# Two-layer adaLN transformer and mixer on one core: the mixer's step size by one Softplus on ScalarE

## The chip, the cores and the metric

The kernel runs on one core of a Trainium2 chip, in one launch. The metric is device microseconds of that core, the median of several runs. The engines are named TensorE (PE), VectorE (DVE), ScalarE (ACT), GpSimd (POOL) and SyncE (SP).

## The reference, cut to what matters

There are 8 sequences ("batches") of 512 tokens of width 128. Layer 0 is attention and a mixture of experts; layer 1 is a mixer (a selective scan) and a second mixture of 8 experts. The mixer, for each batch, with 256 channels and 16 states:

```python
xc = silu(conv(x_in))                                   # (512, 256)
proj = xc @ x_proj_w + x_proj_b                         # (512, 48)
d_raw, Bm, Cm = split(proj, 3)                          # 16 each
delta = softplus(d_raw @ dt_proj_w + dt_proj_b)         # (512, 256)
dA = exp(delta[..., None] * A)
dBx = (delta * xc)[..., None] * Bm[:, :, None, :]
h = dA_t * h + dBx_t                                    # along the tokens
y = sum over n of h[n] * C[n]
```

## The kernel before

Each engine runs one program written out by hand, and the engines wait for each other on counting semaphores. Everything of a batch has its 128 features or channels on the partitions and its 512 tokens along the free axis; the 256 mixer channels are two halves c = 0 and 1. The loop runs over the batches b. In one pass the engines do the attention of batch b, its first experts, its mixer up to the end of the scan, and in the gaps of all this the second layer's experts of batch b - 1 ("behind": batch 0 has none to fill its gaps, and the last batch's come alone, after the loop, as the tail). `early(e)` stands for such pieces outside the scan; in the scan `SCAN_HIDDEN`, `SCAN_OUTPUT` (TensorE), `SCAN_GELU` (ScalarE) and `SCAN_ADD` (VectorE) fix after which step which piece comes. An expert's hidden chunk is one product on TensorE (`hid1`, L602) and one Gelu on ScalarE (`gelu1`, L933). `hid1(n)` waits for the Gelu of chunk n - 2, as two banks take turns.

The mixer's middle part, in which the change lies, goes like this. TensorE makes `proj`, which ScalarE copies out with its bias (L1063). From it start three things. SyncE stores 16 rows of B to DRAM (L398) and loads them back spread over all partitions, two rows (512 KB) in each of 8 DMAs p (L407), into the three slots of `b_wide`; p = 0 goes out at once, p = 1 waits for `dt_l`, because slots 0 and 1 lie in the space of `dt_exp` and `dt_abs`, and p = 2 stands behind it in SyncE's program. VectorE splits B and C into three bfloat16 parts (L1456 to L1458, L1462, L1463: `split_ok`). TensorE makes the input of the softplus for both halves (`dt_mm`, L849).

The softplus is max(z, 0) + ln(1 + exp(-|z|)): ScalarE does Abs (L1066), Exp (L1069) and Ln (L1072) for each half, and VectorE z itself (L1461) and max and sum (L1467). VectorE then has u = delta * xc (L1471).

The scan has 16 steps n of two halves. ScalarE makes the decay factors exp(delta * A) into PSUM (`decays`, L1078; three banks take turns, so decay k waits for scan k - 3). GpSimd makes the injections u * B (L445 for n = 0, L447 after that). VectorE runs the recurrence (L1482, "scan (n, c)") and the product with C (`read_product`, L1162), for which TensorE spreads row n of C (L872, queued behind the scan's wait for `split_ok`). GpSimd (L466) and TensorE (L663) add up the products. After decays 2, 7, 11, 15, 19, 23 and 27 ScalarE loads the Gelu table (L1084), does three Gelus (four after decay 2: chunks 12 to 15) and loads the Exp table again (L1087).

Of the kernel before, what the change touches and what calls it, by code (L numbers as in the profile page):

```python
# [23 lines left out]
ALU = mybir.AluOpType  # L24
# [17 lines left out]
DH = DI // P  # L42
# [28 lines left out]
def build(nc, io, out):  # L71
    ctx = ExitStack()
    with ctx:
# [110 lines left out]
        part = mix_space[0:3 * BC, 14 * T:15 * T]  # L184
        dt_exp, dt_abs, dt_log = conv[0], conv[1], within(8, DH)
        xc = sb("xc", [P, DH, T])
# [3 lines left out]
        split = sb("split", [3 * BC, T], BF16)  # L190
        dt_in, delta, u = (step_space[:, k, :, :] for k in range(3))
        state_sum, y_skip, z = dt_in, delta, u

# [51 lines left out]
        chain_head = signal("chain_head", CHAIN["head"])  # L245
        chain_a = signal("chain_a", CHAIN["act main"])

# [48 lines left out]
        dt_mm = signal("dt_mm", DH)  # L296
        dt_z = signal("dt_z", DH)
        dt_l = signal("dt_l", DH)
        delta_ok = signal("delta_ok", DH)
# [71 lines left out]
        def _(sp):  # L371
# [23 lines left out]
            def spread_rows(b):  # L395

                sp.wait_ge(pr_out.sem, pr_out.at(b, 1))
                sp.dma_start(b_dram[:, :], proj[0:NS, :]).then_inc(b_saved.sem, 16)  # L398
                sp.wait_ge(b_saved.sem, b_saved.at(b, 16))
                rows = b_dram[:, :].unsqueeze(0)  # L400
                for p in range(NS // 2):
                    slot = (p + 2) % 3
                    if p == 1:
                        sp.wait_ge(dt_l.sem, dt_l.at(b, DH))
                    if p >= 3:
                        sp.wait_ge(inj_p.sem, inj_p.at(b, 2 * (p - 3) + 3))
                    sp.dma_start(b_wide[:, slot, :, :], rows[:, 2 * p:2 * p + 2, :].to_broadcast([P, 2, T])  # L407
                                 ).then_inc(b_rows[p % 3].sem, 16)
# [120 lines left out]
        def _(pe):  # L529
# [325 lines left out]
            def scan(b, behind):  # L855
# [9 lines left out]
                pe.wait_ge(split_ok.sem, split_ok.at(b, 1))  # L865
                pe.wait_ge(dt_z.sem, dt_z.at(b, DH))
                if behind:
# [49 lines left out]
        def _(act):  # L917
# [50 lines left out]
            def iteration(b, behind, ahead):  # L968
                mark, _, check = linker(act, chain_a, b)

                def early(e, chunks):
# [22 lines left out]

                nc.scalar.preload_act_table_set("exp_and_others")
                for n in range(UNITS):
# [61 lines left out]
                for c in range(DH):  # L1058
                    act.wait_ge(conv_ok.sem, conv_ok.at(b, c + 1))
                    f(xc[:, c, :], conv[1][:, c, :], ACT.Silu).then_inc(xc_ok.sem, 1)  # L1060
                nc.scalar.preload_act_table_set("natural_log_exp_and_others")
                act.wait_ge(pr_mm.sem, pr_mm.at(b, 1))
                f(proj[:], bank[MISC][0:PR, :], ACT.Identity, bias=w["x_proj_b"][:]).then_inc(pr_out.sem, 1)  # L1063
                for c in range(DH):
                    act.wait_ge(dt_mm.sem, dt_mm.at(b, c + 1))
                    mark(f(dt_abs[:, c, :], bank[HID0_BANK[c]][:], ACT.Abs, bias=w["dt_b"][:, c:c + 1]))  # L1066
                for c in range(DH):
                    act.wait_ge(chain_a.sem, chain_a.at(b, c + 1))
                    mark(f(dt_exp[:, c, :], dt_abs[:, c, :], ACT.Exp, scale=-1.0))  # L1069
                for c in range(DH):  # L1070
                    act.wait_ge(chain_a.sem, chain_a.at(b, DH + c + 1))
                    f(dt_log[:, c, :], dt_exp[:, c, :], ACT.Ln, bias=1.0).then_inc(dt_l.sem, 1)  # L1072

# [7 lines left out]
                for k in range(NS * DH):  # L1081
                    decays(k)
                    if behind and k in SCAN_GELU:
                        nc.scalar.preload_act_table_set("gelu_and_others")  # L1084
                        for m in range(*SCAN_GELU[k]):
                            gelu1(b - 1, m)
                        nc.scalar.preload_act_table_set("natural_log_exp_and_others")  # L1087
                check()

# [21 lines left out]
        def _(dve):  # L1111
# [303 lines left out]
            def iteration(b, behind):  # L1415
# [42 lines left out]
                link(tt(part[low, :], proj[low, :], split[low, :], ALU.subtract))  # L1458
                for c in range(DH):
                    dve.wait_ge(chain_a.sem, chain_a.at(b, c + 1))  # L1460
                    ts(dt_in[:, c, :], bank[HID0_BANK[c]][:], w["dt_b"][:, c:c + 1], None, ALU.add).then_inc(dt_z.sem, 1)  # L1461
                link(cp(split[low, :], part[low, :]))  # L1462
                tt(split[low, :], part[low, :], split[low, :], ALU.subtract).then_inc(split_ok.sem, 1)  # L1463
                for c in range(DH):
                    dve.wait_ge(dt_z.sem, dt_z.at(b, c + 1))
                    dve.wait_ge(dt_l.sem, dt_l.at(b, c + 1))
                    stt(delta[:, c, :], dt_in[:, c, :], 0.0, dt_log[:, c, :], ALU.max, ALU.add).then_inc(delta_ok.sem, 1)  # L1467
                    if c == 1:
                        early(1)
                    dve.wait_ge(delta_ok.sem, delta_ok.at(b, c + 1))  # L1470
                    tt(u[:, c, :], delta[:, c, :], xc[:, c, :], ALU.mult).then_inc(u_ok.sem, 1)  # L1471
                dve.wait_ge(u_ok.sem, u_ok.at(b, DH))
# [53 lines left out]

CHAIN = {"tail": 2, "attend": 15, "main": 32, "head": 16, "act main": 4}
NORM_STEPS = 12
# [81 lines left out]
```

## Time and profile before

| | us |
|---|---|
| median of three runs | 1376.31 |
| lowest and highest | 1374.37, 1383.9 |
| span of the profiled execution, first to last instruction | 1379.8 |
| mean granted TensorE clock in it | 0.950 |

For the profiled execution no time beside its span is listed; the span is 3.5 us above the median of the runs and between their ends. Times in the rows are microseconds from the start of the span; L12 is line 12 of the kernel before. The bracket at the end of a timeline row is how long the engine had been idle and which engine's work ended that. "x3" in a row is three instructions merged.

### The profile page before, as it was taken

To read this page: it belongs to the slowest core of one execution; us is meant where nothing else is said; L and a number is where in the kernel's file an instruction comes from. 1 tells how busy PE (TensorE), PEld (TensorE's weight loads), DVE (VectorE), ACT (ScalarE), POOL (GpSimd) and SP (SyncE) were. 2 spreads that over 40 slices of the span, in tenths; PEclk is the share of its full clock that TensorE was granted. 3 is DMA by queue.
4 is the path that set the end of the run, shared out by engine and by line. 5 is a ranking of instruction groups with operands and counts; after the bars stand their busy time and mean duration, and the time that the engine had idled before them with its cause. 6 is when DMAs were issued, how large, how long until landed. Compare 5 with 4: busy or idle time off the path is not lost. (4 is left out here: it accounts for less than half of the span.)

```text
span 1379.8 us, 19465 instructions
## 1 busy us (share of the span) xinstructions
PE 1207.2 (87%) x6560; PEld 760.5 (55%) x6560; DVE 1037.0 (75%) x2381; ACT 852.2 (62%) x1600; POOL 489.3 (35%) x309
## 2 busy tenths in 40 slices
PE   5974689989998889989999889989899899889698
PEld 3651145655665556555656456655656556555456
DVE  3666977599866997589866997579975998569822
ACT  2634446488646966489565866479664876469332
POOL 0103930078002950069100960049300870029300
PEclk8995579999999999999999999999999999999899
DMA  7101100030001200020001200021000300011000
GB/s 245 70 16 64 60 8 1 16 108 16 16 17 55 69 12 6 16 92 31 17 9 43 88 1 17 16 78 47 16 1 16 109 16 9 1 64 60 8 1 8
DMA packets 18514, 53.22 MB, mean 39 GB/s; under 512 B 4976, under 2 KB 5864, under 8 KB 18032
## 3 DMA queue, kind: packets, MB, share of 16 engines
q1 hardware_dynamic: 16112, 43.40, 9.8%
q0 software_dynamic: 1296, 4.20, 1.0%
q10 hardware_dynamic: 1008, 4.38, 0.8%
q8 instruction: 53, 0.87, 0.3%
q14 instruction: 45, 0.37, 0.1%
HBM read 45.40 MB, written 2.38 MB: 35 GB/s over the span
## 5 line engine op out<-in xcount | busy, mean ns | idle before, releaser
L1482 DVE TENSOR_TENSOR_SCAN probs_T<-bank,probs_T 128x512 f32<-128x512 f32 x256 | 303.9, 1212 | 16.1 <-ACT bank L1078 12.1
L618 PEld LDWEIGHTS bank<-w_w,hidden 128*128 128x128 f32 x2048 | 248.8, 192 | 72.9 <-issue 66.8
L602 PE MATMUL bank<-hT,w_w 128*128 128x512 f32 x512 | 262.9, 629 | 27.1 <-ACT hidden L933 26.2
L447 POOL TENSOR_TENSOR probs_T<-step_space,probs_T 128x1024 f32<-128x1024 f32 x120 | 282.2, 2358 | 5.9 <-DVE probs_T L1482 5.7
L618 PE MATMUL bank<-w_w,hidden 128*128 128x128 f32 x2048 | 251.6, 276 | 2.1 <-DVE expert_sum L1174 1.6
L933 ACT ACTIVATE hidden<-bank,w_b 128x512 f32<-128x512 f32 x256 | 169.6, 686 | 117.5 <-PE bank L602 116.9
L1006 ACT ACTIVATE probs<-bank,row_neg 128x128 f32<-128x128 f32 (+3 forms) x256 | 134.8, 528 | 151.7 <-DVE row_neg L1335 134.8
L1078 ACT ACTIVATE bank<-step_space,a_neg 128x512 f32<-128x512 f32 x256 | 167.8, 683 | 55.0 <-DVE probs_T L1482 36.7
L701 PE MATMUL bank<-k_pad,q_lat 128*128 128x512 f32 (+3 forms) x512 | 185.3, 448 | 5.8 <-DMA k_pad<-xc 5.8
L1335 DVE TENSOR_REDUCE row_neg<-bank 128x1 f32<-128x128 f32 (+3 forms) x256 | 123.5, 487 | 85.1 <-PE bank L703 82.7
L602 PEld LDWEIGHTS bank<-hT,w_w 128*128 128x128 f32 x512 | 89.0, 194 | 153.0 <-ACT hidden L933 97.0
L466 POOL TENSOR_TENSOR step_space<-step_space,probs 128x512 f32<-128x512 f32 x112 | 142.1, 1269 | 66.2 <-DVE probs L1162 66.1
L663 PE MATMUL bank<-probs,w_ident 128*128 128x512 f32 x256 | 146.0, 654 | 9.1 <-DVE probs L1162 9.1
L1162 DVE TENSOR_TENSOR probs<-probs_T,bank 128x1024 f32<-128x1024 f32 x128 | 153.2, 1197 | 0.4 <-PE bank L663 0.3
L711 PE MATMUL bank<-w_ident,probs 128*128 128x128 f32 x640 | 112.7, 278 | 8.6 <-DVE probs_T L1344 7.8
L1174 DVE SCALAR_TENSOR_TENSOR expert_sum<-bank,gates,expert_sum 128x128 f32<-128x128 f32 x256 | 71.4, 341 | 64.0 <-PE bank L618 62.5
L472 POOL TENSOR_TENSOR gated_out<-w_out_w,gate 128x256 f32<-128x256 f32 x8 | 5.8, 722 | 285.0 <-DVE xn L1214 285.0
L711 PEld LDWEIGHTS bank<-w_ident,probs 128*128 128x128 f32 x640 | 69.9, 142 | 59.1 <-issue 31.0
L872 PE MATMUL bank<-split,select 96*128 96x512 bf16 x128 | 52.7, 412 | 48.5 <-DVE probs L1162 45.7
L701 PEld LDWEIGHTS bank<-k_pad,q_lat 128*128 128x128 f32 x512 | 82.4, 200 | 14.8 <-issue 14.0
L982 ACT ACTIVATE probs_T<-bank 128x128 f32<-128x128 f32 (+3 forms) x176 | 73.8, 420 | 18.3 <-PE bank L711 17.5
L445 POOL TENSOR_TENSOR probs_T<-step_space,probs_T 128x512 f32<-128x512 f32 x16 | 23.3, 1459 | 169.3 <-DVE step_space L1471 169.3
(183 smaller groups left out, 1577.6 us busy)
## 6 DMA issues: line engine op xcount, KB each, us to landing
probs_T<-b_rows_dram SPq DMA_DIRECT2D x64, 512.0 KB, 3.7
w_w<-in_w_dram ACTq DMA_DIRECT2D x2, 2048.0 KB, 14.0
k_pad<-xc SPq DMA_DIRECT2D x64, 64.0 KB, 2.0
x_in<-in_x_dram POOLq DMA_DIRECT2D x8, 256.0 KB, 3.3
gate<-gate_rows_dram SPq DMA_DIRECT2D x1, 2048.0 KB, 7.0
out_dram<-x_out POOLq DMA_DIRECT2D x7, 256.0 KB, 2.8
step_space<-in_wmod_dram SPq DMA_DIRECT2D x1, 768.0 KB, 5.6
probs_T<-in_wqT_dram SPq DMA_DIRECT2D x1, 512.0 KB, 4.1
```

The source lines that it names most:

```text
L447: ins = nc.gpsimd.tensor_tensor(inject[:, n % 3, :, :], u[:], row.unsqueeze(1).to_broadcast([P, DH, T]), ALU.mult)
L466: ins = nc.gpsimd.tensor_tensor(state_sum[:, 1, :], state_sum[:, 1, :], read[:, n % 2, 1, :], ALU.add)
L602: mm(hid1_bank(n)[:], w["w1"][:, n // C1, n % C1 * P:(n % C1 + 1) * P], hT[3][:], start=True, stop=True).then_inc(hid1_mm.sem, 1)
L618: ins = mm(to[:, t * P:(t + 1) * P], hidden[:, (e * C1 + c) % (2 * C1), t * P:(t + 1) * P], w["w2"][:, e * C1 + c, :], start=(c == 0), sto ...
L663: mm(bank[SUM_BANK][:], ident[:], read[:, n % 2, 0, :], start=(n == 0), stop=(n == NS - 1)).then_inc(sum_mm.sem, 1)
L701: mm(s[:, 0:(i + 1) * P], q_lat[:, g, i * P:(i + 1) * P], k_pad[:, g, j, 0:(i + 1) * P], start=True, stop=False)
L711: ins = tr(bank[4 + n % 2][:, k * P:(k + 1) * P], probs_ring[:, n % 4, k * P:(k + 1) * P], ident[:])
L933: f(hidden[:, n % (2 * C1), :], hid1_bank(n)[:], ACT.Gelu, bias=w["b1"][:, n:n + 1]).then_inc(hid1_act.sem, 1)
L1006: f(probs_ring[:, n % 4, 0:(i + 1) * P], bank[SCORE_BANK[n % 4]][:, 0:(i + 1) * P], ACT.Exp, bias=row_neg[:, n % 4:n % 4 + 1], accum_out=r ...
L1078: f(decay(k)[:], delta[:, c, :], ACT.Exp, scale=a_neg[:, c, n:n + 1]).then_inc(dec_ok.sem, 1)
L1162: tt(read[:, n % 2, :, :], state[:, n % 2, :, :], bank[C_BANK][:].unsqueeze(1).to_broadcast([P, DH, T]), ALU.mult).then_inc(rd_ok.sem, 1)
L1482: v.tensor_tensor_scan(state[:, n % 2, c, :], decay(DH * n + c)[:], inject[:, n % 3, c, :], 0.0, ALU.mult, ALU.add).then_inc(st_ok.sem, 1)
```

## The change

Delta is one Softplus activation for each half, read from PSUM with the bias, written straight to `delta`. Abs, Exp, Ln, VectorE's z and its max and sum go, with their semaphores. ScalarE loads the set `softplus` where it loaded the one with Exp and Ln, and after the second Softplus `exp_and_others`, which the decays use. The scan's reloads name `exp_and_others` too, so the load at the start of the attention is left out for all batches but the first. VectorE does u of half 0 before the last two operations of the split, then u of half 1, then the adds of `early(1)`, which stood between delta and u of half 1. SyncE's wait for `dt_l` ahead of p = 1 goes, and TensorE's for `dt_z`. The lines are cut to what matters:

```diff
-        dt_exp, dt_abs, dt_log = conv[0], conv[1], within(8, DH)
...
-        dt_in, delta, u = (step_space[:, k, :, :] for k in range(3))
-        state_sum, y_skip, z = dt_in, delta, u
+        state_sum, delta, u = (step_space[:, k, :, :] for k in range(3))
+        y_skip, z = delta, u
...
@@ SyncE, spread_rows
                 for p in range(NS // 2):
                     slot = (p + 2) % 3
-                    if p == 1:
-                        sp.wait_ge(dt_l.sem, dt_l.at(b, DH))
...
@@ TensorE, scan
                 pe.wait_ge(split_ok.sem, split_ok.at(b, 1))
-                pe.wait_ge(dt_z.sem, dt_z.at(b, DH))
...
@@ ScalarE, iteration
-                nc.scalar.preload_act_table_set("exp_and_others")
+                if not behind:
+                    nc.scalar.preload_act_table_set("exp_and_others")
                 for n in range(UNITS):
...
-                nc.scalar.preload_act_table_set("natural_log_exp_and_others")
+                nc.scalar.preload_act_table_set("softplus")
                 act.wait_ge(pr_mm.sem, pr_mm.at(b, 1))
                 f(proj[:], bank[MISC][0:PR, :], ACT.Identity, bias=w["x_proj_b"][:]).then_inc(pr_out.sem, 1)
                 for c in range(DH):
                     act.wait_ge(dt_mm.sem, dt_mm.at(b, c + 1))
-                    mark(f(dt_abs[:, c, :], bank[HID0_BANK[c]][:], ACT.Abs, bias=w["dt_b"][:, c:c + 1]))
-                for c in range(DH):
-                    act.wait_ge(chain_a.sem, chain_a.at(b, c + 1))
-                    mark(f(dt_exp[:, c, :], dt_abs[:, c, :], ACT.Exp, scale=-1.0))
-                for c in range(DH):
-                    act.wait_ge(chain_a.sem, chain_a.at(b, DH + c + 1))
-                    f(dt_log[:, c, :], dt_exp[:, c, :], ACT.Ln, bias=1.0).then_inc(dt_l.sem, 1)
+                    f(delta[:, c, :], bank[HID0_BANK[c]][:], ACT.Softplus, bias=w["dt_b"][:, c:c + 1]
+                      ).then_inc(delta_ok.sem, 1)
+                nc.scalar.preload_act_table_set("exp_and_others")
...
                         for m in range(*SCAN_GELU[k]):
                             gelu1(b - 1, m)
-                        nc.scalar.preload_act_table_set("natural_log_exp_and_others")
+                        nc.scalar.preload_act_table_set("exp_and_others")
...
@@ VectorE, iteration
                 link(tt(part[low, :], proj[low, :], split[low, :], ALU.subtract))
-                for c in range(DH):
-                    dve.wait_ge(chain_a.sem, chain_a.at(b, c + 1))
-                    ts(dt_in[:, c, :], bank[HID0_BANK[c]][:], w["dt_b"][:, c:c + 1], None, ALU.add).then_inc(dt_z.sem, 1)
+
+                def inject_scale(c):
+                    dve.wait_ge(delta_ok.sem, delta_ok.at(b, c + 1))
+                    tt(u[:, c, :], delta[:, c, :], xc[:, c, :], ALU.mult).then_inc(u_ok.sem, 1)
+
+                inject_scale(0)
                 link(cp(split[low, :], part[low, :]))
                 tt(split[low, :], part[low, :], split[low, :], ALU.subtract).then_inc(split_ok.sem, 1)
-                for c in range(DH):
-                    dve.wait_ge(dt_z.sem, dt_z.at(b, c + 1))
-                    dve.wait_ge(dt_l.sem, dt_l.at(b, c + 1))
-                    stt(delta[:, c, :], dt_in[:, c, :], 0.0, dt_log[:, c, :], ALU.max, ALU.add).then_inc(delta_ok.sem, 1)
-                    if c == 1:
-                        early(1)
-                    dve.wait_ge(delta_ok.sem, delta_ok.at(b, c + 1))
-                    tt(u[:, c, :], delta[:, c, :], xc[:, c, :], ALU.mult).then_inc(u_ok.sem, 1)
+                inject_scale(1)
+                early(1)
```

## Rows read from the trace of the kernel before

**Rows 1.** The page: busy time, then groups: busy, mean ns | idle

```profile
PE 1207.2 (87%) x6560; PEld 760.5 (55%) x6560; DVE 1037.0 (75%) x2381; ACT 852.2 (62%) x1600; POOL 489.3 (35%) x309
...
L447 POOL TENSOR_TENSOR probs_T<-step_space,probs_T 128x1024 f32<-128x1024 f32 x120 | 282.2, 2358 | 5.9 <-DVE probs_T L1482 5.7
...
L1162 DVE TENSOR_TENSOR probs<-probs_T,bank 128x1024 f32<-128x1024 f32 x128 | 153.2, 1197 | 0.4 <-PE bank L663 0.3
...
L445 POOL TENSOR_TENSOR probs_T<-step_space,probs_T 128x512 f32<-128x512 f32 x16 | 23.3, 1459 | 169.3 <-DVE step_space L1471 169.3
```

**Rows 2.** Windows, batch 3: length, PE, PEld, DVE, ACT, POOL busy; PEclk, DMA

```profile
604.20:607.60 3.40, 3.40 (x7) 1.52 (x6) 2.42 (x3) 2.60 (x4) 3.40 (x3) 0.51 0.42 154
607.60:660.00 52.40, 48.23 (x231) 29.97 (x229) 51.52 (x58) 45.87 (x58) 45.24 (x26) 1.00 0.12 41
```

**Rows 3.** VectorE's scans by line: what ended the idle time before them

```profile
  ACT bank L1078: 12.1, 7
```

**Rows 4.** Timeline, batch 3, from the copy of proj to scan (1, 1)

```profile
591.45 0.69 ACT L1063 ACTIVATE proj<-bank,w_x_proj_b 112x512 f32<-112x512 f32 x1 [0.16 <-PE bank L843]
...
593.34 0.68 DVE L1458 TENSOR_TENSOR probs_T<-proj,split 32x512 f32<-32x512 f32 x1
593.36 0.69 ACT L1066 ACTIVATE probs_T<-bank,w_dt_b 128x512 f32<-128x512 f32 x1 [1.22 <-PE bank L849]
...
593.74 15.47 SPq L407 DMA_DIRECT2D probs_T<-b_rows_dram  x5
...
594.21 0.69 ACT L1066 ACTIVATE probs_T<-bank,w_dt_b 128x512 f32<-128x512 f32 x1 [0.17 <-PE bank L849]
...
596.62 3.73 PE L618 MATMUL bank<-w_w,hidden 128*128 128x128 f32 x32
...
598.38 1.66 POOL L445 TENSOR_TENSOR probs_T<-step_space,probs_T 128x512 f32<-128x512 f32 x1 [17.19 <-DVE step_space L1471]
...
598.94 1.91 ACT L1078 ACTIVATE bank<-step_space,a_neg 128x512 f32<-128x512 f32 x3 [1.97 <-DVE step_space L1467]
...
600.20 0.38 PE L872 MATMUL bank<-split,select 96*128 96x512 bf16 x1
...
600.87 1.28 ACT L1084 ACT_TABLE_LOAD   x1
...
602.17 1.26 ACT L933 ACTIVATE hidden<-bank,w_b 128x512 f32<-128x512 f32 x2
...
602.91 4.29 PE L602 MATMUL bank<-hT,w_w 128*128 128x512 f32 x6 [2.33 <-ACT hidden L933]
...
607.52 1.91 ACT L1078 ACTIVATE bank<-step_space,a_neg 128x512 f32<-128x512 f32 x3
608.25 1.22 DVE L1482 TENSOR_TENSOR_SCAN probs_T<-bank,probs_T 128x512 f32<-128x512 f32 x1 [1.56 <-ACT bank L1078]
```

**Rows 5.** Timeline, batch 2: the same place at TensorE's full clock

```profile
433.63 0.69 ACT L1063 ACTIVATE proj<-bank,w_x_proj_b 112x512 f32<-112x512 f32 x1 [0.16 <-PE bank L843]
...
445.09 3.03 PE L602 MATMUL bank<-hT,w_w 128*128 128x512 f32 x6 [2.33 <-ACT hidden L933]
...
449.84 1.22 DVE L1482 TENSOR_TENSOR_SCAN probs_T<-bank,probs_T 128x512 f32<-128x512 f32 x1 [0.98 <-ACT bank L1078]
```

**Rows 6.** ScalarE's operations by line and shape: busy us, mean ns | idle before

```profile
L1069 ACT ACTIVATE probs_T<-probs_T 128x512 f32<-128x512 f32 x16 | 9.1, 619 | 0.0
```

**Rows 7.** Timeline, start of the attention that follows batch 3's scan: ScalarE

```profile
662.10 0.37 ACT L1006 ACTIVATE probs<-bank,row_neg 128x128 f32<-128x128 f32 x1 [4.40 <-DVE row_neg L1335]
```

**Rows 8.** DMAs of B issued at 593.5:594, then 596.8:597.15: us to landing

```profile
probs_T<-b_rows_dram SPq DMA_DIRECT2D x1, 512.0 KB, 3.4
...
probs_T<-b_rows_dram SPq DMA_DIRECT2D x1, 512.0 KB, 4.2
```

**Rows 9.** Timeline, batch 0: the copy of proj and the scan that waits

```profile
117.62 0.69 ACT L1063 ACTIVATE proj<-bank,w_x_proj_b 112x512 f32<-112x512 f32 x1 [1.94 <-PE bank L843]
...
132.28 1.22 DVE L1482 TENSOR_TENSOR_SCAN probs_T<-bank,probs_T 128x512 f32<-128x512 f32 x1 [1.08 <-POOL probs_T L447]
```

More of the change, by code:

```diff
@@ L245, in build @@
         chain_head = signal("chain_head", CHAIN["head"])
-        chain_a = signal("chain_a", CHAIN["act main"])
         ln_xn, ln_T, h_ready = (
@@ L296, in build @@
         dt_mm = signal("dt_mm", DH)
-        dt_z = signal("dt_z", DH)
-        dt_l = signal("dt_l", DH)
         delta_ok = signal("delta_ok", DH)
@@ L968, in iteration @@
             def iteration(b, behind, ahead):
-                mark, _, check = linker(act, chain_a, b)
                 def early(e, chunks):
@@ L1086, in iteration @@
                             gelu1(b - 1, m)
-                        nc.scalar.preload_act_table_set("natural_log_exp_and_others")
-                check()
+                        nc.scalar.preload_act_table_set("exp_and_others")
             ln_modulate(0, 0, PRE_BANK)
@@ L1523, in _ @@
                 tt(x_out[:, tiles, :], x_mid[:, tiles, :], expert_out[:, tiles, :], ALU.add).then_inc(last_half, 1)
-CHAIN = {"tail": 2, "attend": 15, "main": 32, "head": 16, "act main": 4}
+CHAIN = {"tail": 2, "attend": 15, "main": 32, "head": 16}
 NORM_STEPS = 12
```

## The prediction

> **What bounds the kernel now.** The page comes first [rows 1]: TensorE is busy for 87% of the span, VectorE for 75%, GpSimd for 35%, so no engine bounds all of it, and each stage has to be read by itself. The windows of batch 3's scan [rows 2] show VectorE busy for 51.5 of the 52.4 us from 607.6 us on, GpSimd for 45.2 and TensorE for 48.2; and on the page VectorE's products, 128 of them, waited 0.4 us in all. What the scans waited for [rows 3] says it of every batch: of 256 scans only seven waited for ScalarE, 12.1 us in sum. From some scan onward, then, the stage is VectorE's own row of work, and what counts is when that scan may start.
>
> Which one it is, and what releases it, the timeline of batch 3 shows [rows 4]. I count from the start of L1063, 591.45 us, as 0. The Abs of the two halves start at 1.9 and 2.8. Exp and Ln follow, then VectorE's max and sum, and only at 7.5 do the decays start, after ScalarE has idled for delta. It does three decays (1.91 us), a table load, Gelus 12 and 13. TensorE had stood for 2.3 us and starts hid1(14) when Gelu 12 is out, at 11.5; Gelus 14 and 15, another load and decay 3 (16.1) follow, and scan (1, 1) starts at 16.8, with decay 3 out. That is one of the seven waits: every batch with experts behind it has one there. In batch 2 [rows 5] the same scan comes 16.21 us after its L1063 and had waited 0.98 us, so without the wait it would come at 15.23. VectorE's own work ahead of it is the same in each batch, and the seven starts add up to 7 x 15.23 + 12.1 = **118.7 us**, 16.96 on the mean. They differ by TensorE's clock: in batch 3 it was 0.51, the lower level of 1.2 GHz, from 604.2 to 607.6 us, right behind TensorE's stand, and full after that [rows 2].
>
> **The change, part by part.** Softplus is not in the trace. From below, it should take no less than the 0.62 us of Exp with a constant bias [rows 6]; from above, the nearest row is Abs, from the same banks with the same bias, 0.69 us [rows 4]. I take 0.69: source, bias and size are those of Abs. The pair then ends where the Abs pair ended, at 3.45.
>
> *ScalarE.* The Exp set's load of 1.28 us comes behind it, and the decays may start at 4.76 in place of 7.49: 2.7 us earlier, although a load is now on the way. The load that goes from the attention's start gives nothing: behind it ScalarE idled for 4.40 us until the scores' maxima came [rows 7]. Decays 0 to 2 end at 6.7, the load at 7.95, Gelus 12 and 13 at 9.2. Here TensorE is late instead: its queue, 32 expert products that start at 596.62 and that the change doesn't touch, lets the first C row start at 8.75 and hid1(14) behind it, 0.38 us long, at 9.15 [rows 4]. Part of ScalarE's lead is lost there. From hid1(14) on I take batch 2, full clock: scan (1, 1) comes 449.84 - 445.09 = 4.75 us behind it [rows 5], at **13.9**.
>
> *The transfer of B.* Injection (0, 0) needs u of half 0 and the row pair p = 0. The first is early: L1458 ends at 2.57, delta 0 is there at 2.6, u is one VectorE operation more. The transfer went out at 2.29 and took 3.4 us [rows 8]: 5.7. It was hidden before, as GpSimd started at 6.93; now it is next late. And p = 1 and p = 2 now go out right behind it. The nearest row for that is p = 1 of the kernel before, with p = 2 right behind it: 4.2 us. I take 4.2, with 3.4 as the lower bound. GpSimd starts at 6.5, does the two half injections, 1.46 us each on the mean, and the one of n = 1, 2.36 us [rows 1]: 11.8. Then 0.1 us, scan (1, 0) of 1.22 and the product of 1.20 us lead to scan (1, 1) at **14.3**. With 3.4 us it would be 13.5, and ScalarE's 13.9 would decide.
>
> *VectorE* loses four operations. What it has left ahead of the scans is u 0, the split's last two, u 1 (each about as L1458's 0.68 us) and four small adds, under 4 us in all from 2.6: done by 6.6, while injection (0, 0) is out at 8 only. So the lost operations save nothing by themselves; they are cover for the transfer. u 0 ahead of the split's end holds `split_ok` up by one operation, but that comes at about 4.6 and TensorE comes for it at 8.75; the wait for delta 0, behind which the split now stands, is 0.03 us. The adds behind u 1 are wanted by TensorE at 8.75 as well.
>
> *SyncE* issues p = 1 and 2 some 2.7 us earlier; nothing else is queued there.
>
> *After scan (1, 1)* all stands to each other as before. Injections 2 to 4 follow the one of n = 1 back to back, out at 11.8 + 3 x 2.36 = 18.9, and scan (4, 0), five scans and two products behind (1, 1), comes at about 22. From then on GpSimd needs 45 us where VectorE needs 52 [rows 2]. TensorE loses its stand of 2.3 us and no work.
>
> The seven batches give 118.7 - 7 x 14.3 = 18.6 us. **Batch 0** has no Gelus; there scan (1, 0) waited for GpSimd, until 132.28 [rows 9]. Its copy of proj ends at 118.3, and 1.6 us later (as in batch 3) the first pair goes out; with 4.2 us GpSimd starts at 124.1 and scan (1, 0) at 124.1 + 2.92 + 2.36 + 0.1 = 129.5: 2.8 us. In all **21.4 us**. The profiled span of 1379.8 us would become 1358.4. It lies 3.5 us above the median of the runs, so from that: 1376.3 - 21.4 = **1355 us**.
>
> *A rule against the added load.* The load starts 0.02 us after the decays and the Gelu 0.02 us after the load [rows 4]: 1.30 us in all. The Trainium skill (ScalarE: Activation LUTs, What ACT_TABLE_LOAD costs) puts a drain of 1.38 us on top of the 1.283 us; the trace disagrees. By the page Gelu 12 would be out at 10.0 in place of 8.6 and hid1(14) would wait for it: scan (1, 1) at 14.8, and 1358 us.
>
> **The rivals.**
>
> *1. TensorE's clock still falls.* The dips cost 118.7 - 7 x 16.21 = 5.2 us. That the one shown came right behind the stand of 2.3 us, which goes, speaks for their going; but TensorE still stands for Gelu 15. If they stay: **1360**.
>
> *2. B's first pair shares its way with both others.* One transfer behind it made 3.4 us into 4.2. With 0.8 us for each of two more shares, 5.8, GpSimd starts at 8.1 and scan (1, 1) comes 7.8 us later, at 15.9; seven times 1.06 us and 1.2 us in batch 0 are 8.6 us: **1368**. The Trainium skill (DMA: Bandwidth & Descriptors, Queues, rings and completion order) lets a queue begin its parts in order and end them out of order, so it doesn't exclude this.
>
> *3. Slower, by the same road.* From 6.9 us to landing on, twice the present time, scan (1, 1) comes later than now (2.29 + 6.9 + 7.8 = 17.0). If the three went one behind the other, the first one finished last, it would land after 10.2 us, each batch would lose 3.3 us, and the time would be **1402**. Against it: p = 1 with a follower was not delayed by a whole transfer of 3.4 us but by 0.8.
>
> *4. The gain doesn't last.* TensorE is busy for 87% of the span. If it bounded the stretch from one scan to the next, the 21 us would come back as waits for it: **1376**. Against it: its work in the scan is shorter than VectorE's [rows 2], and products wait for it for next to nothing [rows 1].
>
> *5. Softplus isn't one short instruction.* If each took 1.5 us more than Abs, decay 3 would come as late as now. The functions in the trace give no sign of that.
>
> **How the numbers follow.** Forecast, 1349 to 1358 with the transfer between 3.4 and 4.6 us: 0.57. Rival 1: 0.14. Rival 2 in all its degrees: 0.10. Rival 4: 0.07. Rivals 3 and 5: 0.05. More than forecast, less clock lost elsewhere too: 0.07. The range leaves out rivals 3, 4 and 5, the far end of 2 and half of the last: 1346 to 1366. A measurement of this kernel can tell about 1% from no change. Faster by over 1%, below 1362.5, is the forecast, rival 1, the last case and a little of 2: 0.8. Within 1%: 0.15. Slower: 0.05.
>
> **What would show it.** In the changed profile: two Softplus rows of 0.69 us and a load right behind them; decays 4.8 us after the copy of proj; injection (0, 0) at 5.7 to 6.5 with a DMA as releaser; no stand of TensorE ahead of hid1(14); the scans' 12.1 us for ScalarE shrunk, with waits for GpSimd beside them; each batch shorter by 2 to 3.5 us. Wrong it would be by a landing of p = 0 far above 4.2 us, a longer Softplus, or scans that start earlier and stand later.

## The result, and the profile after

The changed kernel takes 1357.78 us (four runs, 1356.85 to 1359.15), the kernel before 1377.55 us (1374.37 to 1383.9) in the same sitting: a ratio of 0.9856, 95% interval 0.9828 to 0.9884. Run again twice beside the experiments it gave 0.9815 (0.9791 to 0.9839) and 0.983 (0.9805 to 0.9855). So it is faster by 1.4 to 1.9%, 20 to 27 us; 21.4 us were forecast.

The page of the changed kernel, its busy times and the groups that answer to [rows 1] and [rows 3]. Lines are those of the changed kernel: L1055 copies proj, L1058 is Softplus, L439 and L441 are the injections, L1466 the scans, L1149 the products with C.

```profile
PE 1202.7 (89%) x6560; PEld 758.4 (56%) x6560; DVE 1013.6 (75%) x2349; ACT 837.6 (62%) x1569; POOL 485.4 (36%) x309
...
L1466 DVE TENSOR_TENSOR_SCAN probs_T<-bank,probs_T 128x512 f32<-128x512 f32 x256 | 303.3, 1210 | 16.0 <-POOL probs_T L439 13.4
...
L596 PE MATMUL bank<-hT,w_w 128*128 128x512 f32 x512 | 256.4, 615 | 11.0 <-ACT hidden L926 10.1
...
L1149 DVE TENSOR_TENSOR probs<-probs_T,bank 128x1024 f32<-128x1024 f32 x128 | 153.2, 1196 | 2.2 <-POOL step_space L457 1.5
...
L439 POOL TENSOR_TENSOR probs_T<-step_space,probs_T 128x512 f32<-128x512 f32 x16 | 20.0, 1268 | 159.7 <-DMA probs_T<-b_rows_dram 159.7
```

VectorE lost 23.4 us of busy time, nearly the 22.4 us by which the span fell; whether that is the reason is asked below. The scans wait for GpSimd's first injection in place of ScalarE, and all eight first injections are released by the transfer of B. TensorE's hidden chunks (L596) stood for 11.0 us; before it was 27.1:

```profile
L602 PE MATMUL bank<-hT,w_w 128*128 128x512 f32 x512 | 262.9, 629 | 27.1 <-ACT hidden L933 26.2
```

The timeline of batch 3, for [rows 4]; times in the text are again counted from the start of L1055, 584.77 us:

```profile
584.77 0.69 ACT L1055 ACTIVATE proj<-bank,w_x_proj_b 112x512 f32<-112x512 f32 x1 [0.16 <-PE bank L837]
...
587.05 13.79 SPq L401 DMA_DIRECT2D probs_T<-b_rows_dram  x5
...
587.53 0.69 ACT L1058 ACTIVATE step_space<-bank,w_dt_b 128x512 f32<-128x512 f32 x1 [0.17 <-PE bank L843]
...
588.23 1.28 ACT L1060 ACT_TABLE_LOAD   x1
...
589.53 1.91 ACT L1066 ACTIVATE bank<-step_space,a_neg 128x512 f32<-128x512 f32 x3
589.94 3.73 PE L612 MATMUL bank<-w_w,hidden 128*128 128x128 f32 x32
...
591.06 2.50 POOL L439 TENSOR_TENSOR probs_T<-step_space,probs_T 128x512 f32<-128x512 f32 x2 [16.55 <-DMA probs_T<-b_rows_dram]
...
592.47 2.42 DVE L1466 TENSOR_TENSOR_SCAN probs_T<-bank,probs_T 128x512 f32<-128x512 f32 x2 [1.39 <-POOL probs_T L439]
592.75 1.27 ACT L926 ACTIVATE hidden<-bank,w_b 128x512 f32<-128x512 f32 x2
...
593.51 0.38 PE L865 MATMUL bank<-split,select 96*128 96x512 bf16 x1
...
593.73 2.92 PE L596 MATMUL bank<-hT,w_w 128*128 128x512 f32 x6
...
597.11 1.20 DVE L1149 TENSOR_TENSOR probs<-probs_T,bank 128x1024 f32<-128x1024 f32 x1
597.65 2.68 ACT L1066 ACTIVATE bank<-step_space,a_neg 128x512 f32<-128x512 f32 x4
...
598.37 2.34 DVE L1466 TENSOR_TENSOR_SCAN probs_T<-bank,probs_T 128x512 f32<-128x512 f32 x2
```

Softplus takes 0.69 us like Abs, the load starts 0.01 us behind it, and the decays start at 4.76. GpSimd starts at 6.29, a DMA its releaser. TensorE's first C row comes at 8.74, and hid1(14) follows without a stand. Decay 3 is out at 13.56, product 0 at 13.54, and scan (1, 1) starts at 13.60 without a wait: two chains end together. That is so where the pair of B lands early; in the changed kernel's three runs scan (1, 1) comes at 13.6 to 13.95 in batches 1 to 7, batch 1 of the first run apart, and later than 13.6 where GpSimd started later than 6.4. The DMAs of B issued from 587.0 to 587.1, as in [rows 8], and the windows of the same batch, for [rows 2]:

```profile
probs_T<-b_rows_dram SPq DMA_DIRECT2D x1, 512.0 KB, 3.9
```

```profile
584.77:603.00 18.23, 17.71 (x95) 11.88 (x93) 15.71 (x24) 15.29 (x20) 11.94 (x7) 1.00 0.40 142
```

The first is the first pair of B, from issue to landing; the second is the window. The clock is full from the copy of proj to beyond scan (1, 1), where the kernel before had 0.51 for 3.4 us. What the scans waited for longest, and how often, for [rows 3]:

```profile
  POOL probs_T L439: 13.4, 8
```

To compare runs I use two sums, worked out from the timelines: of the starts of scan (1, 1) after the copy of proj in batches 1 to 7, and of the starts of the last scan in all eight ("stage sum"). What is left, from the last scans to the next copies of proj and the tail, is the same in all runs within 1.6 us on either side of 715.7. But the start, up to the first copy of proj, in which nothing is changed, took 112 to 119 us in the runs, with TensorE's clock low for 17 to 32 us of it. That is most of the scatter between runs of one kernel: 6.6 of the 9.0 us between the shortest and the first profile of the changed kernel.

| run | scan (1, 1), 7 batches | stage sum | first copy of proj | span | ratio to before |
|---|---|---|---|---|---|
| before | 118.6 | 545.7 | 117.6 | 1379.8 | |
| changed kernel | 96.8 | 523.1 | 118.7 | 1357.4 | 0.9856 |
| c_after (the same) | 95.9 | 521.9 | 112.1 | 1348.4 | 0.9815 |
| c2_after (the same) | 96.9 | 523.9 | 118.3 | 1357.5 | 0.983 |
| e1_two_more | 97.2 | 524.7 | 117.6 | 1359.5 | 0.986 |
| e2_four_more | 112.8 | 540.4 | 118.2 | 1374.4 | 0.9988 |
| e10_four_from_psum | 102.4 | 526.3 | 115.5 | 1356.0 | 0.9845 |
| e4_two_undone | 95.7 | 521.7 | 117.9 | 1356.4 | 0.9832 |
| e6_twice | 102.4 | 526.5 | 114.2 | 1354.8 | 0.9868 |
| e5_before_filled | 113.4 | 538.7 | 114.7 | 1369.2 | 0.996 |
| e3_pairs_later | 95.2 | 518.6 | 115.9 | 1348.9 | 0.9823 |
| e11_pairs_later_again | 95.2 | 520.1 | 114.9 | 1350.4 | 0.979 |
| e7_wait_kept | 95.2 | 519.6 | 118.5 | 1353.7 | 0.9829 |
| e9_rows_single | 96.3 | 519.7 | 115.6 | 1350.7 | 0.9806 |

The 95% intervals of the ratios are 0.0015 to 0.0031 wide to either side, so experiments that differ by less than some 4 us from the changed kernel are read by the sums.

### The profile page after: what moved, and what is told of

Same layout as the page of the kernel before. It is cut to its first block and busy times, and to the rows that moved or that the text cites. A ratio compares the mean times of both kernels' runs of the same rounds, so it can differ in the third digit from the quotient of the medians.

```text
span 1357.4 us, 19385 instructions
## 1 busy us (share of the span) xinstructions
PE 1202.7 (89%) x6560; PEld 758.4 (56%) x6560; DVE 1013.6 (75%) x2349; ACT 837.6 (62%) x1569; POOL 485.4 (36%) x309
## 5 line engine op out<-in xcount | busy, mean ns | idle before, releaser
L1466 DVE TENSOR_TENSOR_SCAN probs_T<-bank,probs_T 128x512 f32<-128x512 f32 x256 | 303.3, 1210 | 16.0 <-POOL probs_T L439 13.4
L441 POOL TENSOR_TENSOR probs_T<-step_space,probs_T 128x1024 f32<-128x1024 f32 x120 | 282.2, 2360 | 0.0
L596 PE MATMUL bank<-hT,w_w 128*128 128x512 f32 x512 | 256.4, 615 | 11.0 <-ACT hidden L926 10.1
L596 PEld LDWEIGHTS bank<-hT,w_w 128*128 128x128 f32 x512 | 87.7, 191 | 132.7 <-ACT hidden L926 77.9
L1149 DVE TENSOR_TENSOR probs<-probs_T,bank 128x1024 f32<-128x1024 f32 x128 | 153.2, 1196 | 2.2 <-POOL step_space L457 1.5
L439 POOL TENSOR_TENSOR probs_T<-step_space,probs_T 128x512 f32<-128x512 f32 x16 | 20.0, 1268 | 159.7 <-DMA probs_T<-b_rows_dram 159.7
```

Source lines behind the costliest of these rows:

```text
L441: ins = nc.gpsimd.tensor_tensor(inject[:, n % 3, :, :], u[:], row.unsqueeze(1).to_broadcast([P, DH, T]), ALU.mult)
L596: mm(hid1_bank(n)[:], w["w1"][:, n // C1, n % C1 * P:(n % C1 + 1) * P], hT[3][:], start=True, stop=True).then_inc(hid1_mm.sem, 1)
L1149: tt(read[:, n % 2, :, :], state[:, n % 2, :, :], bank[C_BANK][:].unsqueeze(1).to_broadcast([P, DH, T]), ALU.mult).then_inc(rd_ok.sem, 1)
L1466: v.tensor_tensor_scan(state[:, n % 2, c, :], decay(DH * n + c)[:], inject[:, n % 3, c, :], 0.0, ALU.mult, ALU.add).then_inc(st_ok.sem, 1)
```

## The experiments

The theory: the stage from the copy of proj to the last scan is bounded from scan (1, 1) on by VectorE, and the change's gain is that this scan starts 3 us earlier, because delta and with it the decays come earlier; the transfer of B is the next to be late. The edits below are cut to what matters; in the kernels the added operations are written out one by one. The rivals: VectorE's removed work is the gain; TensorE's clock is; or the gain is smaller than it could be because of the transfers behind the first one.

**VectorE's work put back: e1_two_more, e2_four_more.**

```diff
                 inject_scale(1)
+                for _ in range(2):      # 4 in e2_four_more
+                    link(stt(state_sum[:, 0, :], xc[:, 0, :], 0.0, res_gate[:, 0, :], ALU.max, ALU.add))
                 early(1)
```

> The changed kernel with two idle VectorE operations of 128x512 added in each batch, between u of half 1 and the four adds (about 1.4 us a batch, 11.5 us in all; their output is read by nobody). Theory (the gain is the earlier start of scan (1, 1), VectorE's lost operations were only cover): VectorE stands 1.35 to 1.66 us for the first injection ahead of scan (0, 0) in each batch (2.9 in batch 1, 13.4 us in all), and the two go into that: 0 to 1 us slower than the changed kernel, about 1358 us. Rival (VectorE's busy time fell by 23.4 us and the span by 22.4, so the removed VectorE work is the gain): half of it comes back, 11 us, about 1369 us.

> As before it, with four such operations (2.9 us a batch, 23 us in all). Theory: the cover of 13.4 us is used up and the rest shows, 23 - 13.4 = 10 us, about 1368 us, with scan (0, 0) released by VectorE itself. Rival of removed work: all 23 us come back, about 1380 us.

Measured: e1_two_more 0.986 (0.9834 to 0.9885) and a stage sum 0.8 to 2.7 us above those of the changed kernel's three runs, a little more than the 0 to 1 expected; e2_four_more 0.9988 (0.997 to 1.0006), 17.3 us above the first of them. The first says that removing VectorE's work was not the gain: 11 us of it are back and cost 0.8 to 2.7. Its scans' wait for the first injections:

```profile
  POOL probs_T L439: 2.0, 2
```

The 13.4 us went to 2.0. The second is far from the theory's 10 us, and by its time alone nearer to the rival's 23. Its timeline of batch 2 shows where the rest comes from:

```profile
439.02 0.69 DVE L1457 SCALAR_TENSOR_TENSOR step_space<-xc,res_gate 128x512 f32<-128x512 f32 x1
...
439.13 3.39 POOL L439 TENSOR_TENSOR probs_T<-step_space,probs_T 128x512 f32<-128x512 f32 x2 [16.99 <-DMA probs_T<-b_rows_dram]
439.75 1.64 DVE L1458 SCALAR_TENSOR_TENSOR step_space<-xc,res_gate 128x512 f32<-128x512 f32 x1
...
442.70 0.38 PE L865 MATMUL bank<-split,select 96*128 96x512 bf16 x1 [1.41 <-DVE expert_sum L1161]
...
443.98 0.69 ACT L926 ACTIVATE hidden<-bank,w_b 128x512 f32<-128x512 f32 x1 [2.33 <-PE bank L596]
```

The fourth operation took 1.64 us where the third took 0.69, and GpSimd's pair of half injections 3.39 us where the changed kernel needed 2.50: both run from 439.75 on. The adds came late, TensorE stood 1.41 us for them, and Gelu 14 waited 2.33 us. In batch 3 two operations were stretched, TensorE stood 2.35 us, and the clock fell to 0.50 behind that, from 601.6 to 605.0 (and once more in batch 5):

```profile
601.60:605.00 3.40, 3.40 (x6) 1.16 (x5) 3.40 (x8) 1.53 (x3) 3.40 (x3) 0.50 0.43 154
```

Batch 1 of the same run is the counter-example. There the pair of B came late (see the end), GpSimd started at 7.82 after the copy of proj in place of 6.3 to 6.7, and the four operations were all but done:

```profile
282.65 0.69 DVE L1458 SCALAR_TENSOR_TENSOR step_space<-xc,res_gate 128x512 f32<-128x512 f32 x1
...
283.11 2.59 POOL L439 TENSOR_TENSOR probs_T<-step_space,probs_T 128x512 f32<-128x512 f32 x2 [18.07 <-DMA probs_T<-b_rows_dram]
...
284.65 0.38 PE L865 MATMUL bank<-split,select 96*128 96x512 bf16 x1 [0.45 <-DVE expert_sum L1161]
```

None of them is stretched, TensorE stands 0.45 us, and scan (1, 1) comes at 15.08, where the changed kernel with the same late pair has 14.97; in the other six batches it comes at 15.6 to 17.3.

**The same number of operations, one operand from PSUM: e10_four_from_psum.**

```diff
+                    link(stt(state_sum[0:PR, 0, :], bank[MISC][0:PR, :], 0.0, xc[0:PR, 0, :], ALU.max, ALU.add))   # four times
```

> As e2_four_more, but the four added VectorE operations take one operand from PSUM in place of two from SBUF. Theory (in e2_four_more two of the added operations met GpSimd's first injections and both took up to 1 us longer, as both engines read two operands from SBUF): no added operation over 0.8 us, GpSimd's pair of half injections at 2.5 us, TensorE's stand for the adds under 1 us, and the eight stages from the copy of proj to the last scan some 12 us longer in sum than the changed kernel's, where e2_four_more was 17 us longer. Rival (the stretch has to do with the place, not with the operands): the same 17 us and operations of 1.6 us.

Batch 2's timeline:

```profile
430.65 2.51 POOL L439 TENSOR_TENSOR probs_T<-step_space,probs_T 128x512 f32<-128x512 f32 x2 [16.66 <-DMA probs_T<-b_rows_dram]
430.87 0.69 DVE L1457 SCALAR_TENSOR_TENSOR step_space<-bank,xc 112x512 f32<-112x512 f32 x1
...
431.60 0.69 DVE L1458 SCALAR_TENSOR_TENSOR step_space<-bank,xc 112x512 f32<-112x512 f32 x1
...
433.60 0.38 PE L865 MATMUL bank<-split,select 96*128 96x512 bf16 x1 [0.45 <-DVE expert_sum L1161]
```

Every added operation takes 0.69 us, the pair of injections 2.51, TensorE stands 0.45 us. The stage sum is 3.2 us above the changed kernel's first run, where 12 were expected and 17.3 measured with two operands from SBUF: the meeting of VectorE and GpSimd, with the stands and dips that follow from it, cost 14 us there. The 12 us expected were too many: scan (1, 1) came at 14.6 in each of the seven batches, 0.8 us later than in the changed kernel on the mean of its three runs, though 2.8 us of VectorE's work had been added, and some 0.35 us come back behind it (see the next experiment). The ratio is 0.9845 (0.9825 to 0.9866). These operations are on 112 partitions in place of 128; two operands from SBUF on 112 were not tried, but batch 1 above parts the meeting from the place without that difference.

**ScalarE's chain longer: e6_twice.**

```diff
                 for c in range(DH):
                     act.wait_ge(dt_mm.sem, dt_mm.at(b, c + 1))
+                    f(delta[:, c, :], bank[HID0_BANK[c]][:], ACT.Softplus, bias=...).then_inc(once.sem, 1)
+                for c in range(DH):
+                    act.wait_ge(once.sem, once.at(b, c + 1))
                     f(delta[:, c, :], bank[HID0_BANK[c]][:], ACT.Softplus, bias=...)
```

> The changed kernel with each half's Softplus done twice, 1.4 us more on ScalarE ahead of delta. Theory (decay 3 and VectorE reach scan (1, 1) together): decay 3 comes 1.1 us later, as 0.3 us of ScalarE's lead over TensorE's first hidden chunk covers the rest, so seven batches are 1.1 us longer and batch 0 is not: 8 us slower than the changed kernel, about 1366 us. Rival (the transfer of B and GpSimd alone decide): no change, 1358 us.

```profile
582.10 0.69 ACT L1059 ACTIVATE step_space<-bank,w_dt_b 128x512 f32<-128x512 f32 x1 [0.17 <-PE bank L844]
...
589.22 3.03 PE L597 MATMUL bank<-hT,w_w 128*128 128x512 f32 x6 [0.76 <-ACT hidden L927]
...
593.97 1.22 DVE L1471 TENSOR_TENSOR_SCAN probs_T<-bank,probs_T 128x512 f32<-128x512 f32 x1 [0.81 <-ACT bank L1071]
```

That is batch 3, 579.34 us its copy of proj: scan (1, 1) at 14.63, waiting 0.81 us for decay 3. It is 1.0 us later than in the changed kernel, where 1.1 were expected, for 1.4 us more on ScalarE; TensorE stands 0.76 us for Gelu 12. The wait is there in all seven. But the stage sum is only 3.4 us above the changed kernel's, not 8. In each batch some 0.35 us come back after scan (1, 1): the last scan comes 51.82 us behind it, as before the change, where the changed kernel's seven need 52.06 to 52.25. What the changed kernel loses there is the third product's wait for GpSimd's first sum, L457, which follows four injections without a gap, here in batch 2:

```profile
438.05 9.30 POOL L441 TENSOR_TENSOR probs_T<-step_space,probs_T 128x1024 f32<-128x1024 f32 x4
...
447.31 1.26 POOL L457 TENSOR_TENSOR step_space<-probs 128x512 f32<-128x512 f32 x1
...
448.77 1.22 DVE L1149 TENSOR_TENSOR probs<-probs_T,bank 128x1024 f32<-128x1024 f32 x1 [0.26 <-POOL step_space L457]
```

In batches 2, 3 and 5 this product starts 0.20 us after the end of that sum, 5.9 to 6.0 us behind scan (1, 1), where it is 5.61 in the same batches of e6_twice and of the kernel before, in which the sum ends 0.56 us or more ahead of it. And batch 1 of the changed kernel was late for another reason (below). So the theory holds for scan (1, 1), and my sum left out that something was already being given back behind it.

**The order of u and the table load: e4_two_undone.**

```diff
                 link(tt(part[low, :], proj[low, :], split[low, :], ALU.subtract))
-                inject_scale(0)
                 link(cp(split[low, :], part[low, :]))
                 tt(split[low, :], part[low, :], split[low, :], ALU.subtract).then_inc(split_ok.sem, 1)
+                inject_scale(0)
                 inject_scale(1)
...
-                if not behind:
-                    nc.scalar.preload_act_table_set("exp_and_others")
+                nc.scalar.preload_act_table_set("exp_and_others")
```

> The changed kernel with two of its parts undone: u of half 0 stands behind the split's last two operations again, and the Exp table is loaded again at each attention's start. Theory: no change beside the changed kernel (both are hidden: u of half 0 then ends at 4.6 us after the copy of proj, the transfer of B lands at 6.3; ScalarE idles 4 us behind the load). If the place of u mattered, the first injection would come up to 1.1 us later, 9 us in all; if the table load did, 1.3 us a batch, 9 us.

The stage sum is 521.7, beside the 521.9 to 523.9 of the changed kernel; 0.9832 (0.9812 to 0.9852) against its 0.9815 (0.9791 to 0.9839) on the same chip. What is left behind the last scans is 716.8 us, 1.2 us more than the changed kernel's highest. So neither part gives the 9 us that it was priced at; a gain of about 1 us from them can't be told from nothing here.

**TensorE's clock: e5_before_filled.** The kernel before, with the stand of 2.3 us filled:

```diff
                     if n >= 1:
                         sum_first(n - 1)
+                    elif behind:
+                        for _ in range(2):
+                            mm(bank[SUM_BANK][:], ident[:], res_gate[:, 0, :], start=True, stop=True)
                     expert_pieces(n)
```

> The kernel before with TensorE's stand ahead of hid1(14) filled by two products of 128x512 that nobody reads, so that TensorE does not stand for 2.3 us. Theory (the fall of TensorE's clock right behind it goes with the stand): the seven waits of scan (1, 1) shrink from 12.1 us to about 7 x 1.0 = 7 us, and the kernel is 4 to 5 us faster than before; that is the clock's share of the change's gain. Rival (the dips come with something else, the change's gain is all operations): no change, dips where they were. If the two products (1.7 us) ran into the time in which Gelu 12 is out, each batch would be longer by that; they should be done 0.6 us ahead of it.

In batch 3 TensorE's products follow each other up to a stand of 0.61 us, and scan (1, 1) comes 16.20 us after the copy of proj, 585.56, in place of 16.8. The clock of the window that answers to the one of 604.2 to 607.6 in [rows 2] is 1.00:

```profile
594.53 1.88 PE L877 MATMUL bank<-res_gate,w_ident 128*128 128x512 f32 x4
...
597.01 3.03 PE L602 MATMUL bank<-hT,w_w 128*128 128x512 f32 x6 [0.61 <-ACT hidden L936]
...
601.76 2.34 DVE L1485 TENSOR_TENSOR_SCAN probs_T<-bank,probs_T 128x512 f32<-128x512 f32 x2 [0.97 <-ACT bank L1081]
```

```profile
598.30:601.70 3.40, 3.40 (x21) 2.21 (x20) 2.42 (x3) 3.20 (x5) 3.40 (x3) 1.00 0.43 153
```

All seven batches give 16.20, and the scans waited 6.8 us for ScalarE in place of 12.1. The kernel is 0.996 (0.9945 to 0.9975) of before, 5.5 us. In the sum of the seven scans (1, 1) it is 5.2 us, and that is the clock's share of their 21.8: the change takes away the stand, and with it the dip in the five batches that had one.

The stage sum fell by 7.0 us. The other 1.8 are batch 0's, in which this experiment changes nothing: its scan (1, 1) came 15.12 us after the copy of proj in place of 16.92. TensorE's clock was 0.50 all through that stretch in the profile before, and in this one it was full for the first 7 us behind the copy of proj. The products for the softplus, before and here:

```profile
118.36 3.78 PE L849 MATMUL bank<-proj,w_dt_w 112*128 112x512 f32 x4 [0.78 <-ACT proj L1063]
```

```profile
115.46 1.98 PE L849 MATMUL bank<-proj,w_dt_w 112*128 112x512 f32 x4 [0.78 <-ACT proj L1066]
```

In the changed kernel batch 0 has 13.53 with the clock at 0.50 and 13.42 at 0.73: there the transfer of B comes later than delta either way. So 1.8 of the 3.4 us that batch 0 gained hang on a low clock in the profile before.

**The transfers behind the first: e3_pairs_later, e7_wait_kept, e9_rows_single.**

```diff
                 for p in range(NS // 2):
                     slot = (p + 2) % 3
+                    if p == 1:
+                        sp.wait_ge(dec_ok.sem, dec_ok.at(b, 1))       # e3, e9, e11
+                        sp.wait_ge(delta_ok.sem, delta_ok.at(b, DH))  # e7, in its place
...
+                    if p == 0:                                        # e9: one row each
+                        for r in range(2):
+                            sp.dma_start(b_wide[:, slot, r:r + 1, :], rows[:, r:r + 1, :].to_broadcast([P, 1, T])
+                                         ).then_inc((b_rows[0] if r else b_first).sem, 16)
...
+                if n == 0:                                            # e9, GpSimd
+                    pool.wait_ge(b_first.sem, b_first.at(b, 16))
```

> The changed kernel with SyncE waiting for the first decay ahead of row pair p = 1, so that p = 0 has no transfer behind it for its first 3.2 us. Theory: p = 0 lands after 3.4 us in place of 3.9 to 4.1, the first injection starts 0.5 us earlier, but scan (1, 1) stays at 13.6 us after the copy of proj, since decay 3 is out at 13.56 too; VectorE's third product no longer waits for GpSimd's first sum (1.5 us in all): 0 to 2.5 us faster than the changed kernel. Rival (GpSimd alone bounds now): each batch 0.5 us shorter, 4 us faster. Second rival (the landing of 4.0 us has nothing to do with the transfers behind it): no change anywhere.

> The changed kernel with SyncE's wait ahead of row pair p = 1 kept, now for delta of both halves, which comes 1.2 us after p = 0 has gone out (in the run with the wait for the first decay it was 3.2 us). Theory (the followers slow p = 0 where they overlap it): the landing is between 3.6 and 4.0 us, and the time between those two, 1 to 4 us faster than the changed kernel. Rival (only a follower issued at once matters): as good as the wait for the decay, 5 us.

> The changed kernel with the wait for the first decay ahead of p = 1, and the first row pair sent as two transfers of one row (256 KB) each, the injection of n = 0 waiting for the first alone. Theory (with the transfer out of the way, decay 3 bounds scan (1, 1) at 13.6 us after the copy of proj): row 0 lands some 0.5 us or more earlier than the pair, VectorE's stand ahead of scan (0, 0) shrinks, ScalarE's wait ahead of scan (1, 1) grows by as much, and the seven batches stay at 13.6; only batch 0 gets up to 0.5 us shorter: no measurable difference from e3_pairs_later. Rival (the transfer bounds the seven batches): each shorter by the 0.5 us, 4 us.

> e3_pairs_later again, beside the changed kernel on the same chip: the eight stages 3 to 4.5 us shorter in sum than the changed kernel's, time 2 to 5 us less.

The first pair of e3_pairs_later's batch 2 landed after 3.6 us, of its batch 3 after 3.7. Over all batches it took 3.3 to 3.7 in this run and 3.3 to 3.8 in the repeat, as in the kernel before (3.3 to 3.8), and 3.8 to 4.4 in the changed kernel's three runs. The landing, the scans' waits and batch 2's scan (1, 1), 13.60 us behind its copy of proj at 422.83:

```profile
probs_T<-b_rows_dram SPq DMA_DIRECT2D x1, 512.0 KB, 3.6
```

```profile
  POOL probs_T L441: 9.5, 8
  ACT bank L1068: 2.5, 7
```

```profile
436.43 2.34 DVE L1468 TENSOR_TENSOR_SCAN probs_T<-bank,probs_T 128x512 f32<-128x512 f32 x2 [0.37 <-ACT bank L1068]
```

Seven times scan (1, 1) stays at 13.60 or 13.61, now with waits for ScalarE of 2.5 us in sum, and the last scan comes 51.82 to 51.97 us behind it: most of the 0.35 us are back. The stage sums are 518.6 and 520.1, 2 to 5 us below the changed kernel's. That gain is spread: what comes back behind scan (1, 1), batch 0, the batches in which the pair of B was late enough to decide, and batch 1. In time, e11_pairs_later_again took 1347.69 us (0.979, 0.9769 to 0.9811) beside the changed kernel's 1353.79 (0.983, 0.9805 to 0.9855) on one chip; the intervals overlap, and 3.3 of the 7.1 us between the two profiles are the start. e7_wait_kept, with the follower held back by 1.2 us only, landed its pairs after 3.4 to 4.0 us and has 519.6 and 0.9829 (0.9805 to 0.9853): the sums don't tell it from e3, and its time isn't below c_after's, where 1 to 4 us less were expected.

e9_rows_single brought the first injection forward once more, and changed nothing for the seven batches (batch 1 apart): in batch 3, copy of proj at 579.07, it starts at 5.79, the stand ahead of scan (0, 0) is 0.88 us, and the wait for ScalarE ahead of scan (1, 1), again at 13.60, 0.56:

```profile
584.86 2.50 POOL L450 TENSOR_TENSOR probs_T<-step_space,probs_T 128x512 f32<-128x512 f32 x2 [16.05 <-DMA probs_T<-b_rows_dram]
...
586.26 2.42 DVE L1477 TENSOR_TENSOR_SCAN probs_T<-bank,probs_T 128x512 f32<-128x512 f32 x2 [0.88 <-POOL probs_T L450]
...
592.67 2.34 DVE L1477 TENSOR_TENSOR_SCAN probs_T<-bank,probs_T 128x512 f32<-128x512 f32 x2 [0.56 <-ACT bank L1077]
```

Its ratio is 0.9806 (0.9783 to 0.9828). ScalarE's chain, which TensorE's queue holds, bounds these batches now, as expected.

**The changed kernel beside the others: c_after, c2_after.**

> The changed kernel itself, beside the others on the same chip: 1357.8 us within 2 us, 19 to 22 us faster than before.

> The changed kernel again on the same chip as the three others: between 1352 and 1358 us; how far its start up to the first copy of proj (112 to 119 us in the runs so far) moves its time.

c_after took 1352.07 us, c2_after 1353.79. The first is 3.7 us below what I expected at the least, and 25.5 us faster than before by its ratio, where 19 to 22 were expected; its first copy of proj came at 112.1 us in the profile. The second is within its range.

## Why the prediction was right

- **Softplus at 0.69 us and its load.** Right to 0.01 us, both; the decays start at 4.76 as worked out. The trace's rule held, no drain behind a load, not the page's 1.38 us (the Trainium skill, ScalarE: Activation LUTs, What ACT_TABLE_LOAD costs): the decay starts 0.02 us after the load. The working of that rule counted one drain, for the added load; Gelu 12 has two loads ahead of it, so by the page it would have come later still.
- **TensorE's queue.** The C row was put at 8.75 and came at 8.74; hid1(14) at 9.15 and came at 8.96, its first product overlapping the C row's end. Scan (1, 1) by ScalarE: 13.9 forecast, 13.6 measured. That the queue holds a part of ScalarE's lead e6_twice showed: 1.4 us more there, 1.0 us here.
- **The transfer of B.** 4.2 us forecast, 3.8 to 4.2 measured in the first run and up to 4.4 in the repeats; it is the releaser in all eight batches. That its followers slow it was shown by holding them back (3.3 to 3.8); rival 2's even shares, 5.8 us, and rival 3's queueing, 10.2 us, did not occur.
- **The injections, mis-sized.** I took 2 x 1.46 us, the mean of the kernel before. There the first one ran beside VectorE's max and sum and took 1.66; in the changed kernel VectorE is done and both take 1.27, 2.50 the pair. In batches 4 and 5, where GpSimd starts at 6.57 and 6.53 as forecast, scan (1, 1) comes at 13.73 and 13.69 in place of 14.3: 0.46 us are the pair, the rest is that the scan and the product start before the one ahead has ended. In the other batches the pair of B was also earlier than the 4.2 us forecast. Together this made the term of the seven batches 21.8 us in place of 18.6, although batch 1 lost 1.4. e2_four_more brought the stretch back. For batch 0 the same: 3.4 us in place of 2.8, but only against a batch 0 at low clock (e5_before_filled: 1.6).
- **VectorE's lost operations as cover.** Right: e1_two_more. The prediction left 1.4 us between VectorE's end, 6.6, and the injection, 8; the two operations of e1_two_more, 1.4 us, went into it, and the four of the next two runs did not. What it costs to go beyond depends on the operands and on whether GpSimd has begun: 3.2 or 17.3 us.
- **Nothing given back after scan (1, 1).** Wrong by 0.2 to 0.4 us a batch. I held injections 2 to 4 against scan (4, 0), but not GpSimd's first sum, queued behind them, against the third product.
- **Rival 1, the clock.** Priced right (5.2 us; e5_before_filled gave 5.2 in the sum of scan (1, 1)), and rejected rightly: none of batches 1 to 7 has the dip there in the changed kernel's three runs.
- **The sum.** The stage sum fell by 22.6 us, and from the first copy of proj to the end the profile is shorter by 23.4; the start of this profile was 1.0 us longer, so its span fell by 22.4. The 21.4 us forecast stands on two errors of opposite sign, 3.8 us too little for the scans' start and 2.5 us (7 x 0.36) too much for what is given back, and on batch 0, whose gain hangs on its clock; by the medians of the same sitting the gain is 19.8 us, and the kernel before alone ran between 1374.4 and 1383.9. The path, its waits and the order in which they end were right; two sizes were not, and that the total came so close is in part luck.

## What to carry to other kernels

A shorter chain gives what the next chain leaves: work out, for the place where the wait ends, each engine's arrival after the change, the transfers' among them, and stop at the latest. A fall in busy time that equals the gain proves nothing; put the work back as idle operations and look. When a stand of TensorE goes, look for a clock dip behind it: here it was a quarter of the gain in the seven batches. And a wait that is removed because it is no longer needed may have been spacing transfers.

## What the runs showed of the hardware

- VectorE operations with two operands from SBUF and GpSimd's two-operand multiplications stretch each other where they meet: 0.69 to 1.64 us on VectorE, a pair from 2.50 to 3.39 us on GpSimd. An operation that had begun 0.46 us before GpSimd did kept its 0.69 us (batch 1 of e2_four_more). With one operand from PSUM VectorE kept its 0.69 us beside GpSimd. Four operations a batch cost 17.3 us one way and 3.2 us the other.
- A transfer of 512 KB with two others issued right behind it, 0.4 to 0.5 us apart, landed after 3.8 to 4.4 us, with the next one 3.2 us later after 3.3 to 3.8.
- In the kernel before, TensorE's clock, otherwise full in batches 1 to 7 of the scan, went to 0.50 or 0.51 for 3.4 us right behind stands of 2.33 us in five of seven batches, and in none where the stand was filled. Why the two other stands of the same length had no dip stays open.
- The store of B to DRAM took 2.9 us in batch 1 of the changed kernel's first run, where it takes 1.6; a transfer of the instruction queue ran in the same stretch. Its first injection came 1.5 us late, which cost 1.4 us in that batch. All fourteen profiles have this transfer of 16 KB at this place. In four of them (the changed kernel's first run, e1_two_more, e2_four_more and e9_rows_single) it begins 0.88 to 0.94 us after the store is issued, and the store takes 2.9 to 3.5 us; in the ten others it begins 1.08 to 1.18 us after it, and the store takes 1.6. That speaks for the transfer as the cause; moving it was not tried.
